# Second attention: the probabilities divided by their sums on GpSimd, the output projected without transposes

## The reference

```python
sim = jnp.einsum('bhid,bhjd->bhij', q, k) * SCALE      # q, k normalised per head
sim = jnp.where(m, sim, max_neg)
attn = jax.nn.softmax(sim, axis=-1)                    # divided by the sum over j
out = jnp.einsum('bhij,bhjd->bhid', attn, v)
out = out.transpose(0, 2, 1, 3).reshape(b, n, INNER)   # 100 tokens x 512
out = jnp.einsum('bne,ed->bnd', out, Wo)               # 512 -> 256
return stable_layernorm(out, g_out)                    # divides by the row's maximum first
```

## Time and profile before

| | us |
|---|---|
| median of 3 runs | 841.67 (839.44 to 844.37) |
| the profiled execution, its own time | 843.17 |
| its span, first to last instruction | 841.0 |
| busy in the span: PE, DVE, ACT, POOL | 755.5, 394.8, 421.8, 240.3 |
| mean granted TensorE clock | 0.945 of 2.4 GHz |

### The profile page before, as it was taken

One profiled execution on the slowest core, in us unless ns is written; L12 is line 12 of the kernel. 1 busy time (PEld: TensorE's weight loads), 2 busy tenths in 40 slices (PEclk: granted clock), 3 DMA queues, 4 the chain that ended last, 5 costly groups with the idle time before them and its releaser, 6 DMA issues.

```text
span 841.0 us, 16036 instructions
## 1 busy us (share of the span) xinstructions
PE 755.5 (90%) x5001; PEld 594.1 (71%) x5002; DVE 394.8 (47%) x1222; ACT 421.8 (50%) x968; POOL 240.3 (29%) x258
## 2 busy tenths in 40 slices
PE   3997999999962999979999989996879999999996
PEld 2775666666551888756767656664659999999996
DVE  4223666777552111137777755456653343333432
ACT  2665766666631323234555597774414444444442
POOL 4111333333206000012121100000216766757562
PEclk9997999999955999988999999999689999999998
DMA  5125000000064487110010010000014443433431
GB/s 127 42 79 186 2 2 2 1 2 1 2 193 151 130 293 265 36 52 23 18 36 18 0 44 1 1 2 1 1 48 154 116 133 115 134 114 115 133 115 39
DMA packets 58408, 61.48 MB, mean 73 GB/s; under 512 B 5905, under 2 KB 51191, under 8 KB 58363
## 3 DMA queue, kind: packets, MB, share of 16 engines
q1 hardware_dynamic: 55388, 57.36, 22.3%
q10 hardware_dynamic: 1952, 1.91, 0.8%
q0 software_dynamic: 1024, 1.64, 0.7%
HBM read 53.68 MB, written 7.22 MB: 72 GB/s over the span
## 4 chain that ended last, share of the span: by engine, by line
PE 78%; DVE 11%; issue 3%; ACT 3%; DMA 2%; POOL 1%; SPq 1%; DVEq 0%; POOLq 0%; ACTq 0%
PE psum L627 5%; PE psum L635 5%; PE psum L1868 5%; PE psum L1870 5%; PE psum L1869 5%; PE psum L649 5%; PE psum L1032 4%; PE psum L1045 4%; PE psum L548 3%; PE psum L1387 3%; PE psum L1883 3%; PE psum L1884 3%; PE psum L1882 3%; PE psum L562 3%; PE psum L1408 2%
## 5 line engine op out<-in xcount | busy, mean ns | idle before, releaser
L1992 DVE TENSOR_TENSOR kT_all<-kT_all 128x400 f32<-128x400 f32 x60 | 36.6, 610 | 114.5 <-ACT kT_all L1926 106.5
L1868 PE MATMUL psum<-xT_high,we_high 128*128 128x400 f32 x240 | 83.2, 347 | 0.0
L1870 PE MATMUL psum<-xT_high,we_low 128*128 128x400 f32 x240 | 82.8, 345 | 0.0
L1869 PE MATMUL psum<-xT_low,we_high 128*128 128x400 f32 x240 | 82.6, 344 | 0.0
L729 POOL TENSOR_SCALAR probs<-probs 100x722 f32<-100x722 f32 x64 | 50.5, 790 | 110.3 <-DVE probs L737 110.3
L1965 POOL TENSOR_TENSOR h_low<-v_all,h_high 128x400 fp32r<-128x400 f32 x60 | 63.2, 1053 | 65.3 <-ACT h_high L1930 65.2
L737 DVE TENSOR_SCALAR_CACHE_REDUCE probs<-psum 100x361 f32<-100x361 f32 x128 | 63.1, 531 | 25.2 <-PE psum L627 25.2
L1956 POOL TENSOR_TENSOR we_low<-v_all,we_high 128x512 fp32r<-128x512 f32 (+1 forms) x61 | 66.7, 1104 | 19.1 <-ACT we_high L1915 15.5
L694 ACT ACTIVATE probs<-probs,negmax 100x361 f32<-100x361 f32 x128 | 69.0, 588 | 6.3 <-POOL probs L729 4.0
L1926 ACT ACTIVATE kT_all<-psum 128x400 f32<-128x400 f32 x60 | 30.0, 501 | 52.5 <-PE psum L1870 52.5
L699 ACT ACTIVATE probsT<-psum 128x400 f32<-128x400 f32 x64 | 32.3, 504 | 42.3 <-PE psum L635 42.3
(11 more groups left out here) (349 smaller groups left out, 1654.4 us busy)
## 6 DMA issues: line engine op xcount, KB each, us to landing
v_all<-in_L_ffn_W_dram SPq DMA_DIRECT2D x16, 1024.0 KB, 7.8
kT_all<-coefT_dram SPq DMA_DIRECT2D x30, 400.0 KB, 3.5
v_all<-in_L_ffn_Wg_dram SPq DMA_DIRECT2D x31, 128.0 KB, 2.1
v_all<-in_L_ffn_Wu_dram SPq DMA_DIRECT2D x31, 128.0 KB, 2.2
v_all<-in_L_ffn_Wd_dram SPq DMA_DIRECT2D x31, 128.0 KB, 2.1
ctx_nat<-in_ctx_dram SPq DMA_DIRECT2D x17, 192.0 KB, 2.4
xs_dram<-zeros SPq DMA_DIRECT2D x1, 2048.0 KB, 7.7
ys_dram<-zeros SPq DMA_DIRECT2D x1, 1792.0 KB, 12.6
```

The costliest lines, as they stand in the source:

```text
L1868: nc.tensor.matmul(ps, we_high[p][:, col], xT_high[:, c, tok], start=(c == 0), stop=False)
L1869: nc.tensor.matmul(ps, we_high[p][:, col], xT_low[:, c, tok], start=False, stop=False)
L1870: last = nc.tensor.matmul(ps, we_low[p][:, col], xT_high[:, c, tok], start=False, stop=(c == 1))
```

## The change

- GpSimd gets a function `pool_attend1`, called ahead of `pool_shared`: for each pair it waits for the reciprocals, multiplies the two heads' probabilities, 100 x 362 each, in place by them, and releases `divided`.
- PE's transposes(n) wait for `divided` of n instead of `exp_done` of n.
- DVE's normalise goes. In its place invert_sums(n) takes the reciprocal of the two sums of pair n, once per pair. DVE looks three pairs ahead (AHEAD1 = 3): its loop is masked_max(n+3), invert_sums(n+1), and at s = 2 scale_by_top of the batch before.
- The two finish transposes and the copy to `o_tokT` go. finish_project takes `oT` directly; it stands at s = 1.
- The sums lie in the columns of the pair's buffer, n % NPB, and exps(n) waits until those of n-4 have been inverted.

```diff
@@ -376,11 +376,8 @@
             s.probsT_ready = sem("L1_probsT_ready")
             s.attended = sem("L1_attended")
             s.out_taken = sem("L1_out_taken")
-            s.tok_ready = sem("L1_tok_ready")
             s.inv_ready = sem("L1_inv_ready")
-            s.normalised = sem("L1_normalised")
-            s.tokT_in_psum = sem("L1_tokT_in_psum")
-            s.tokT_ready = sem("L1_tokT_ready")
+            s.divided = sem("L1_divided")
             s.projected = sem("L1_projected")
             s.added = sem("L1_added")
             s.stats_ready = sem("L1_stats_ready")
@@ -1375,6 +1372,7 @@
                                      scale=q1_scale[:, 0:1]).then_inc(qT1_stored, 1)
 
     PAIRS1 = 4
+    AHEAD1 = 3
     N1 = B * PAIRS1
 
     def pe_attend1(pe):
@@ -1389,7 +1387,7 @@
             last.then_inc(A1.scores_ready, 1)
 
         def transposes(n):
-            pe.wait_ge(A1.exp_done, n + 1)
+            pe.wait_ge(A1.divided, n + 1)
             for t in range(3):
                 for hh in range(2):
                     last = nc.tensor.transpose(pT_ps[0:rows1[t], t, hh * NQ:(hh + 1) * NQ],
@@ -1411,27 +1409,13 @@
             if s == PAIRS1 - 1:
                 last.then_inc(A1.attended, 1)
 
-        def finish_transpose(b):
+        def finish_project(b):
             pe.wait_ge(A1.out_taken, b + 1)
             if b > 0:
                 pe.wait_ge(A1.added, b)
-            for g in range(4):
-                last = nc.tensor.transpose(y_ps[0:NQ, g * P:(g + 1) * P], oT[:, g, :], ident[:, :])
-            last.then_inc(A1.tok_ready, 1)
-
-        def finish_transpose_back(b):
-            pe.wait_ge(A1.normalised, b + 1)
             for c in range(4):
-                last = nc.tensor.transpose(y_ps[:, c * NQ:(c + 1) * NQ], o_tok[:, c * P:(c + 1) * P],
-                                           ident[0:NQ, 0:NQ])
-            last.then_inc(A1.tokT_in_psum, 1)
-
-        def finish_project(b):
-            pe.wait_ge(A1.tokT_ready, b + 1)
-            for c in range(4):
-                last = nc.tensor.matmul(y_ps[0:NQ, 0:D], o_tokT[:, c, :], wo1[:, c, :], start=(c == 0), stop=(c == 3))
+                last = nc.tensor.matmul(y_ps[0:NQ, 0:D], oT[:, c, :], wo1[:, c, :], start=(c == 0), stop=(c == 3))
             last.then_inc(A1.projected, 1)
-        finish = {0: finish_transpose, 1: finish_transpose_back, 2: finish_project}
 
         for n in range(LOOK):
             scores(n)
@@ -1440,22 +1424,20 @@
             if n + LOOK < N1:
                 scores(n + LOOK)
             b, s = n // PAIRS1, n % PAIRS1
-            if b > 0 and s in finish:
-                finish[s](b - 1)
+            if b > 0 and s == 1:
+                finish_project(b - 1)
             weighted(n)
-        for s in range(3):
-            finish[s](B - 1)
+        finish_project(B - 1)
 
     def act_attend1(act):
         def exps(n):
-            b, s = n // PAIRS1, n % PAIRS1
-            if s == 0 and b >= 2:
-                act.wait_ge(A1.normalised, b - 1)
             act.wait_ge(A1.max_ready, n + 1)
+            if n >= NPB:
+                act.wait_ge(A1.inv_ready, n - NPB + 1)
             for hh in range(2):
                 row = probs[:, n % NPB, hh, 0:NK1]
                 last = nc.scalar.activation(row, row, ACT.Exp, bias=negmax[:, n % NPB, hh:hh + 1], scale=-1.0,
-                                            accum_out=sums[:, b % 2, 2 * s + hh:2 * s + hh + 1])
+                                            accum_out=sums[:, 0, 2 * (n % NPB) + hh:2 * (n % NPB) + hh + 1])
             last.then_inc(A1.exp_done, 1)
 
         def take(n):
@@ -1467,11 +1449,6 @@
         def finish_take(b):
             act.wait_ge(A1.attended, b + 1)
             nc.scalar.activation(oT[:, :, :], o_ps, ACT.Copy).then_inc(A1.out_taken, 1)
-
-        def finish_takeT(b):
-            act.wait_ge(A1.tokT_in_psum, b + 1)
-            nc.scalar.activation(o_tokT[:, :, :], y_ps[:, 0:4 * NQ].rearrange("p (c n) -> p c n", c=4), ACT.Copy
-                                 ).then_inc(A1.tokT_ready, 1)
 
         act.wait_ge(mask_null, 3)
         act_mask_bias(act, 0, 0)
@@ -1481,8 +1458,6 @@
             b, s = n // PAIRS1, n % PAIRS1
             if b > 0 and s == 0:
                 finish_take(b - 1)
-            if b > 0 and s == 2:
-                finish_takeT(b - 1)
             if s == 1 and b + 1 < B:
                 act_mask_bias(act, b + 1, 1 - b % 2)
             take(n)
@@ -1490,7 +1465,15 @@
                 exps(n + AHEAD)
         finish_take(B - 1)
         act_std_before_last1(act)
-        finish_takeT(B - 1)
+
+    def pool_attend1(pool):
+        for n in range(N1):
+            pool.wait_ge(A1.inv_ready, n + 1)
+            for hh in range(2):
+                k = 2 * (n % NPB) + hh
+                row = probs[:, n % NPB, hh, 0:NK1]
+                last = nc.gpsimd.tensor_scalar(row, row, inv_sums[:, k:k + 1], 1.0, ALU.mult, ALU.mult)
+            last.then_inc(A1.divided, 1)
 
     def dve_attend1(dve):
         def masked_max(n):
@@ -1507,14 +1490,12 @@
                     op0=ALU.add, op1=ALU.min, scale=1.0, scalar=FLT_MAX, accum_out=negmax[:, k, hh:hh + 1])
             last.then_inc(A1.max_ready, 1)
 
-        def normalise(b):
-            dve.wait_ge(A1.tok_ready, b + 1)
-            nc.vector.reciprocal(inv_sums[:, 0:8], sums[:, b % 2, 0:8]).then_inc(A1.inv_ready, 1)
-            dve.wait_ge(A1.inv_ready, b + 1)
-            nc.vector.tensor_tensor(o_tok[:, :].rearrange("q (h e) -> q h e", e=HD1),
-                                    y_ps[0:NQ, :].rearrange("q (h e) -> q h e", e=HD1),
-                                    inv_sums[:, 0:8].unsqueeze(2).broadcast_to([NQ, 8, HD1]), ALU.mult
-                                    ).then_inc(A1.normalised, 1)
+        def invert_sums(n):
+            dve.wait_ge(A1.exp_done, n + 1)
+            if n >= NPB:
+                dve.wait_ge(A1.divided, n - NPB + 1)
+            k = 2 * (n % NPB)
+            nc.vector.reciprocal(inv_sums[:, k:k + 2], sums[:, 0, k:k + 2]).then_inc(A1.inv_ready, 1)
 
         def scale_by_top(b):
             dve.wait_ge(A1.projected, b + 1)
@@ -1528,18 +1509,18 @@
             nc.vector.bn_stats(stats[:, b + 1, :], z_all[:, b + 1, :]).then_inc(A1.stats_ready, 1)
 
         dve.wait_ge(mask_null, 3)
-        for n in range(AHEAD):
+        for n in range(AHEAD1):
             masked_max(n)
+        invert_sums(0)
         for n in range(N1):
             b, s = n // PAIRS1, n % PAIRS1
-            if b > 0 and s == 1:
-                normalise(b - 1)
-            if b > 0 and s == 3:
+            if n + AHEAD1 < N1:
+                masked_max(n + AHEAD1)
+            if n + 1 < N1:
+                invert_sums(n + 1)
+            if b > 0 and s == 2:
                 scale_by_top(b - 1)
-            if n + AHEAD < N1:
-                masked_max(n + AHEAD)
         dve_before_last1(dve)
-        normalise(B - 1)
         dve_while_projecting1(dve)
         scale_by_top(B - 1)
 
@@ -2052,6 +2033,7 @@
             pool_split_weights1(pool)
             pool_project1(pool)
             pool_mask_clear(pool)
+            pool_attend1(pool)
             pool_shared(pool)
             pool_experts1(pool)
 
```

## The result

The changed kernel takes 900.87 us (median of 4 runs, 898.91 to 905.42) against 841.71 of the kernel before beside it: a ratio of 1.071, 95% interval 1.066 to 1.076. It is slower by 59 us. The forecast was 907 with a range of 872 to 924.

A forecast was written before the change was run, and what follows sets the result against it. The prediction took TensorE's instruction stream to bound the second attention. Profiled 843.17 us plus 65.4 (+38.0 order: 2.1 + 39.0 - 1.4 - 1.65; +27.4 clock) gave 908.6, less 1.5 to the median, 907; range 872 to 924.

The forecast's parts named there:

- The circle: Second attention: each pair's transposes wait through scores, maxima, reciprocal and division for the previous pair's transposes, 4.16 us per pair.
- Rival 3: Second attention: VectorE reaches the reciprocal early enough, TensorE stays the bound at 10.52 us per batch, 834 us; chance 0.04.
- Circle at full clock: From the first transposes to those of pair 29: 29 circles of 4.16 us, 120.6 against 81.66, +39.0 us.
- rival 4: Second attention: a milder circle of 3.2 to 3.9 us per pair through overlaps, 850 to 870 us; chance 0.05.
- GpSimd's price: Division of a pair's two heads on GpSimd: between 0.79 and 1.47 us, the middle 1.13 taken.
- Count of circles: Second attention's loop: 22 circles without a projection (plain) and seven with one.
- the drain: Last two pairs, from pair 29's transposes until oT is ready: 7.0 us against 8.46, -1.4 us.
- Clock: TensorE's clock falls between projections and returns in one: 13.4 us for plain circles, 14 for projection ones, +27.4 together.
- Rival 2: Clock low except in projections (933 us), or division at the two-input price (903 or 930); chance 0.1.
- Start and end: Second attention: first transposes +2.1 us later; from oT to the last scale_by_top 1.65 us saved.

The follow-up runs named there:

- Experiment 1: Changed kernel with invert_sums(n+1) moved ahead of masked_max(n+3) in VectorE's queue: 842.64 us, ratio 1.000 to the kernel before.
- experiment 3: Changed kernel without GpSimd's multiplications, the transposes waiting for the reciprocal alone: 844.3 us, ratio 1.003.
- experiment 6: Changed kernel with scores, exponentials and reciprocals also one pair further ahead, maxima still three, and the root ahead of the last oT: 836.89 us, ratio 0.993.
- experiment 2: Changed kernel with AHEAD1 = 2 instead of 3, so maxima two pairs ahead: 836.69 us, ratio 0.994.
- experiment 4: Changed kernel with five filling matmuls in every plain pair that still has scores to make and once behind the first three scores: 874.44 us, ratio 1.039.
- experiment 11: Experiment 10 plus three filling matmuls ahead of the last projection: 831.5 us, ratio 0.989.
- experiment 9: Experiment 1 with scale_by_top moved between the reciprocal and the maximum in VectorE's loop: 838.4 us, ratio 0.995.
- experiment 7: Experiment 2 plus ScalarE's square root and its table load ahead of the last copy of oT: 836.46 us, ratio 0.991.
- experiment 8: Experiment 7 plus ScalarE's two copies of a pair releasing the weighted matmuls one by one: 834.76 us, ratio 0.989.
- experiment 10: Experiment 8 plus five filling matmuls once, behind the first three scores: 830.1 us, ratio 0.987.

## Why the prediction was right, step by step

**Mechanism: right, and shown.** The circle transposes, scores, maxima, reciprocal, division, transposes is in every plain pair of the timeline. Experiment 1 breaks it by swapping two calls and gives the 59 us back; experiment 3 takes its dearest member out and it stays a circle, of 2.70 us; experiment 6 shows that the number 3 alone is harmless. Rival 3 (TensorE stays the bound, 834) fails for the kernel as it is; with the order put right experiment 2 comes near it (836.7).

**Circle at full clock: 3.92, predicted 4.16.** Term by term from the timeline above: 0.67 to the scores (0.67), 0.86 for them (0.85), 1.12 for the division (1.13), 0.06 to the transposes (0.06). Between scores' end and GpSimd's start lie 1.21 (547.45 to 548.66), where the prediction had 1.16 + 0.20 + 0.08 = 1.44. This is the mis-sized term. The 1.16 were taken from the first maxima up to the exponential, and so contained 0.16 from the scores' end to the first maximum, where the circle has 0.05, and the 0.08 of reading the maximum, while the reciprocal starts at 548.41 together with that reading: up to it the circle has 0.96. The reciprocal was counted as 0.20 and takes 0.16. Together 4.16 for 3.92, and 29 x 0.24 = 7.0 us. It is an overlap of the kind that rival 4 named. GpSimd's price, bracketed between 0.79 and 1.47, came out at 1.12, next to the middle that was taken; since no row spoke for the middle, that hit is luck.

**Count of circles.** There are 23 plain ones and 6 with a projection (pairs 5, 9, ..., 25), not 22 and 7. The seventh projection runs at pair 29, in the drain. There it costs 0.86 (the pair takes 3.06 where 2.2 were counted), which is most of why the drain gave back 0.3 and not 1.4.

**Clock: 24.2, predicted 27.4, with its parts off in both directions.** A slow plain circle takes 5.11 to 5.12, 1.19 over a fast one (1.22 predicted). Seven of the 23 are slow in full (pairs 1 to 4, 12, 20 and 28) and three a little (4.59, 4.07, 4.01), against 11 of 22 predicted: 9.2 us for 13.4. The six projection pairs take 6.99, 6.21, 6.87, 6.10, 6.76 and 6.05, 39.0 together, where experiment 4 has them at 4.02: 14.9 us for 14. The half of the circles and the 6.2 us for a pair with a projection were estimates that no row fixed; that their sum came within 3.2 us is in part luck. (Rival 2 names 2.9 us more for each projection and adds up 3.7.)

The clock falls between projections and is back at the end of each of the six projections in the loop, as forecast; in the first batch it stayed low from pair 0 to the projection in pair 5. But a projection isn't needed for its return. It fell once more in pair 27 and was back in pair 28, ahead of the next transposes, while TensorE was idle:

```profile
629.20:630.36 1.16, 0.00 (x1) 0.00 (x1) 0.00 (x0) 0.00 (x0) 1.16 (x3) 0.99 0.00 0
```

TensorE's work before that, from 625.25 on, had run at 0.50.

On this the Trainium skill, "TensorE: Matmul & The Clock Gate", has two rules, and the prediction weighed them. Section "HAM oscillation — how this bites in real kernels" asks for longer gaps of TensorE than this loop ever has in its middle. The longest here is 1.62 us, and the granted clock of 0.50 from 549.84 to 554.95 contradicts the rule as a condition for losing the clock. Section "A second HAM failure mode: psum-queue depth-cycling" says of another kernel that short, frequent idle spells between groups of matmuls do it. The trace agrees: gaps of 1.62 us, one in each pair of 3.92, came before the fall at 547.3.

**Start and end.** The start came 0.1 below its term. At the end of the stage the square root's table and the additions were late instead of the projection, and 1.7 us were saved where 1.65 had been worked out; experiment 11 shows again that a projection there lies beside them.

**Sum.** The profiled times differ by 58.2 (901.35 - 843.17), 7.2 less than the +65.4 forecast: -6.5 for the circles at full clock (-7.0 for the way from the scores to the division, +0.6 for six projection pairs at 4.02, rounded), -3.2 for the clock, +1.1 for the drain, -0.2 for the start and the end, and +1.6 that lies outside the stage.

## What to carry to other kernels

When work is added between two engines, write down for each in-order queue which pair it is working for; if an instruction for a pair far ahead stands in front of one for the next pair, the look-ahead is lost and all latencies add up into one circle per pair. That cost 32 us here at full clock, and swapping two calls or changing one number took it away. Then look at the share of time in which TensorE idles: the gaps themselves cost a further 24 us through its clock, and a few filling matmuls in them (here 1.2 us per pair) tell both costs apart in one run. Experiment 4 is that run: its 32.5 us are left when the clock is held.

## What the runs showed of the hardware beyond that

- An instruction of VectorE can start under the reading of the previous one's accumulators: the reciprocal starts at 548.41, at the same time as the 0.08 us of that reading.
- GpSimd multiplies 100x362 fp32 by a factor per partition in 572 ns (562 to 573 over 64), 1.58 ns a column; with constant factors 722 columns took 790, 1.09 ns a column.
- In the loop of gaps TensorE was busy 2.27 of 3.92 us in the pair at 542.00, all at a granted clock of 1.00. The clock fell 1.4 us into the next pair, while TensorE was working on the scores: 0.92 from 546.59 to 547.45, then 0.50. That pair still took 3.92, since its slow weighted values (1.27 for 0.74) lie beside the circle. With fillers, busy 14.12 of 15.77 us, TensorE kept the clock for all of 110 us.
- At the start of the stage TensorE idle for 2.42 us (the changed kernel and experiments 1 and 9) or 1.89 (experiments 2, 7 and 8) was followed, one or two groups of matmuls later, by work at half clock; after 1.29 (experiment 4), 1.18 (experiment 3, without a filler) and 0.76 (experiments 10 and 11) it was not. Experiments 3 and 10 support that these idle times are the cause. They are not all of it: at the end of the stage the same 1.49 us of idle TensorE was followed by half clock in experiment 8 and by full clock in experiment 10, and what made that difference no run shows.
